# A graph network's edge counts: the first two source one-hots of seven groups made by ScalarE instead of VectorE

## The reference

```
adj  = zeros(N, N).at[src, dst].set(1)              # attention mask
cnt  = number of edges src->dst, plus the self loops # aggregation
h  = relu(layernorm(x))
x  = x + softmax(mask((h Wq + bq)(h Wk + bk)^T / sqrt(512), adj)) (h Wv + bv)
h  = relu(layernorm(x))
h  = agg(h W1 + b1);  h = relu(batchnorm(h));  h = agg(h W2 + b2)
x  = x + h            # agg(y)[s] = sum over edges s->d of dinv[s] dinv[d] y[d]
```

## Time and profile before

| what | value |
|---|---|
| three timed runs | 309.1, 309.43, 310.83 us (median 309.43) |
| profiled execution, its own time | 309.07 us |
| its span (first to last instruction) | 307.2 us |
| busy in the span | PE 295.4 us (96%), DVE 210.1 (68%), ACT 143.6 (47%), POOL 56.5 (18%) |
| source one-hots L674 | 149, 349 ns each, 44.3 us of DVE |
| chunk matmuls L1021 | 36.5 us of PE |
| granted clock of PE | 9 in all 40 slices, mean 1.000 |

### The profile page before, as it was taken

The page is one execution under the profiler, slowest core; times in us unless marked ns, Lnnn a source line. Parts: engine busy times, 40 slices in busy tenths (PEclk is TensorE's granted clock), DMA queues, the critical chain, the costliest instruction groups (busy, mean ns, idle before and its releaser), DMA issues.

```text
span 307.2 us, 4787 instructions
## 1 busy us (share of the span) xinstructions
PE 295.4 (96%) x1339; PEld 227.5 (74%) x1345; DVE 210.1 (68%) x472; ACT 143.6 (47%) x245; POOL 56.5 (18%) x94
## 2 busy tenths in 40 slices
PE   8999879899999999999999999999999999999995
PEld 6778346466565788888888888887888888878884
DVE  3798999999998648766757484667344388276311
ACT  3999924444346726635454445537623035343000
POOL 5352450000000340032121411203010044100000
PEclk9999999999999999999999999999999999999999
DMA  7815040000600308544452825223102000000221
GB/s 265 298 45 164 7 133 0 1 0 3 200 5 3 69 2 210 98 102 75 100 120 53 154 51 104 51 54 68 34 19 51 1 2 0 0 2 0 109 99 68
DMA packets 42312, 21.66 MB, mean 71 GB/s; under 512 B 35761, under 2 KB 36017, under 8 KB 42289
## 3 DMA queue, kind: packets, MB, share of 16 engines
q1 hardware_dynamic: 41744, 20.33, 26.5%
q10 hardware_dynamic: 544, 1.05, 0.9%
HBM read 10.88 MB, written 2.10 MB: 42 GB/s over the span
## 4 chain that ended last, share of the span: by engine, by line
PE 81%; DVE 7%; issue 4%; DVEq 3%; DMA 2%; ACT 1%; SPq 0%; ACTq 0%
PE ps L955 19%; PE ps L957 18%; PE ps L956 18%; PE ps L1205 10%; PE ps L1128 8%; PE ps L1021 7%; DVE src_oh L674 3%; DMA qk_raw<-L_gnn_Wq_in 2%; DVE dst_oh L676 1%; DVEq L674 1%; PE ps L989 1%; DVE T L775 0%; DVEq L666 0%; DVE smx L779 0%; DVE p L787 0%
## 5 line engine op out<-in xcount | busy, mean ns | idle before, releaser
L674 DVE TENSOR_SCALAR src_oh<-iota,ecol 128x512 f16 x149 | 44.3, 349 | 4.5 <-issue 3.4
L1021 PE MATMUL ps<-src_oh,dst_oh 128*128 x143 | 36.5, 382 | 6.2 <-DVE dst_oh L676 5.0
L1021 PEld LDWEIGHTS ps<-src_oh,dst_oh 128*128 x149 | 14.4, 104 | 25.7 <-issue 16.6
L1128 PE MATMUL ps<-cnt,qh 128*128 128x512 f32 x128 | 30.1, 391 | 0.3 <-ACT cnt L544 0.3
L1205 PE MATMUL ps<-qh,cnt 128*128 128x512 f32 x128 | 29.3, 390 | 0.0
L446 ACT ACTIVATE cnt<-ps 64x512 int16<-64x512 f32 x32 | 18.9, 591 | 20.7 <-PE ps L1035 20.3
L1128 PEld LDWEIGHTS ps<-cnt,qh 128*128 128x128 f32 x128 | 23.9, 188 | 5.6 <-DVE qh L834 0.7
L1205 PEld LDWEIGHTS ps<-qh,cnt 128*128 128x128 f32 x128 | 24.0, 188 | 5.2 <-DVE vb L936 0.3
L957 PE MATMUL ps<-v,pT 128*128 128x512 f32 x64 | 25.0, 390 | 0.0
L955 PE MATMUL ps<-hT,qh 128*128 128x512 f32 x64 | 24.9, 390 | 0.0
L955 PE MATMUL ps<-v,pT 128*128 128x512 f32 x64 | 24.9, 389 | 0.0
(11 more groups left out here) (179 smaller groups left out, 660.4 us busy)
## 6 DMA issues: line engine op xcount, KB each, us to landing
xt<-x_in SPq DMA_DIRECT2D x16, 256.0 KB, 3.3
out<-xt SPq DMA_DIRECT2D x8, 256.0 KB, 2.1
qk_raw<-L_gnn_Wk_in ACTq DMA_DIRECT2D x2, 512.0 KB, 4.7
qk_raw<-L_gnn_Wq_in SPq DMA_DIRECT2D x2, 512.0 KB, 6.5
wB_raw<-L_gnn_Wv_in SPq DMA_DIRECT2D x2, 512.0 KB, 8.5
wB_raw<-L_gnn_W_in SPq DMA_DIRECT2D x2, 512.0 KB, 3.8
w_raw<-L_gnn_W_in SPq DMA_DIRECT2D x2, 512.0 KB, 4.3
bias_row<-L_gnn_b_in SPq DMA_DIRECT2D x2, 256.0 KB, 3.7
```

The costliest lines, as they stand in the source:

```text
L674: dve.tensor_scalar(src_oh[:, bass.ds(slot, 1), j, :].rearrange("p a n -> p (a n)"), iota[:, :], ecol[:, bass.ds(c + j, 1)], None, ALU.is_ ...
L1021: m = pe.matmul(ps[:, i % 2, :], dst_oh[:, bass.ds(slot, 1), :, j].rearrange("p a n -> p (a n)"), src_oh[:, bass.ds(slot, 1), j, :].rearra ...
L1128: m = pe.matmul(bank(g), qh[:, d, a, c * P:(c + 1) * P], cnt[:, d, n * HALF:(n + 1) * HALF], start=(d == 0 and a == 1), stop=last)
```

## The change

For groups 3 to 9 the two source one-hots of the straight round are no longer made by DVE. POOL negates the source column once (`ncol`) and copies the two columns that the group needs to a fixed place (`lead_col`, after reading the group's first chunk from `lohi`). ACT makes |iota - source| for each of the two chunks, and then relu(1 - that) over both, which is 1 where they are equal and 0 elsewhere, into `lead_oh` (two buffers, in the place that `adj` takes later). It does so for group i+1 between `hi_of` of group i's items and `counts(i)`. PE waits for it (`lead_made`) before group i+1's first round. DVE still makes that round's target one-hot.

```
+ACT_LEADS = 3
+ACT_LAST = 10
...
-    adj = sb("adj", [P, ADJ, N], I16)
+    adj, lead_oh = shared([("adj", [P, ADJ, N], I16)], [("lead_oh", [P, 2, LEAD, HALF], BF16)])
+    hold("region_adj", 4)
...
+    ncol = sb("ncol", [P, NCH + PAD], F32)
+    lead_col = sb("lead_col", [P, NW, LEAD], F32)
+    ones = sb("ones", [P, 1], F32)
...
 # POOL
+        pool.memset(ones[:, :], 1.0)
...
+        def lead_columns(i):
+            bounds = pool.value_load(lohi[0:1, ORDER[i]:ORDER[i] + 1], min_val=256, max_val=257 * NCH)
+            pool.tensor_copy(lead_col[:, i, :], ncol[:, bass.ds(bounds & (NCH - 1), LEAD)]).then_inc(S["lead_cols"], 1)
...
-        pool.wait_ge(S["ecol_ready"], 1)
+        pool.wait_ge(S["ecol_ready"], 2)
...
         ln1(6)
+        pool.tensor_scalar(ncol[:, :], ecol[:, :], -1.0, 0.0, ALU.mult,
+                           ALU.add).then_inc(S["ncol_ready"], 1)
+        pool.wait_ge(S["ncol_ready"], 1)
+        pool.wait_ge(S["bounds_ready"], 1)
+        for i in range(ACT_LEADS, ACT_LAST):
+            lead_columns(i)
         for i in range(8, NW):
             targets_of(i)
...
 # ACT
+        def lead_onehots(i):
+            n = i - ACT_LEADS + 1
+            act.wait_ge(S["lead_cols"], n)
+            for j in range(LEAD):
+                act.activation(lead_oh[:, i % 2, j, :], iota[:, :], ACT.Abs,
+                               bias=lead_col[:, i, j:j + 1]).then_inc(S["lead_dist"], 1)
+            act.wait_ge(S["lead_dist"], LEAD * n)
+            act.activation(lead_oh[:, i % 2, :, :], lead_oh[:, i % 2, :, :], ACT.Relu, bias=ones[:, 0:1],
+                           scale=-1.0).then_inc(S["lead_made"], LEAD)
...
+            if ACT_LEADS <= i + 1 < ACT_LAST:
+                lead_onehots(i + 1)
             counts(i)
...
 # DVE
-            for j in range(count):
+            for j in range(count if src else 0):
...
-            chunks_of(i, first, LEAD)
+            chunks_of(i, first, LEAD, not ACT_LEADS <= i < ACT_LAST)
...
 # PE
+                              lead_oh[:, i % 2, j, :] if first and ACT_LEADS <= i < ACT_LAST else
                               src_oh[:, bass.ds(slot, 1), j, :].rearrange("p a n -> p (a n)"), start=first and j == 0,
...
+            if ACT_LEADS <= i < ACT_LAST:
+                pe.wait_ge(S["lead_made"], LEAD * (i - ACT_LEADS + 1))
```

More of the change, by code:

```diff
@@ L159, in gnn_kernel @@
     x_sums x_means x_squares ln_scale ln_coef h_ready item_ps item_hi item_lo uw_ready hw_second fill_ready
-    onehots onehots_used c_done c16 loops_added adj_in0 adj_in1 adj_in2 adj_in3
+    ncol_ready lead_cols lead_dist lead_made onehots onehots_used c_done c16 loops_added adj_in0 adj_in1 adj_in2 adj_in3
     deg_ready degm_ready degm_ps flag_ready dinv_ready
@@ L666, in bounds_of, with chunks_of @@
             return dve.value_load(lohi[0:1, ORDER[i]:ORDER[i] + 1], min_val=256, max_val=257 * NCH)
-        def chunks_of(i, c, count):
+        def chunks_of(i, c, count, src=True):
             k = dve.snap(made, min_val=0, max_val=ROUNDS)
```

## The result

The changed kernel takes 307.77 us, the kernel before 310.48 beside it (medians of 12 runs each): ratio 0.9926, 95% interval 0.9912 to 0.9940, so 2.3 us faster by the ratio (1.9 to 2.7 by its interval); 2.4 was forecast. A later comparison on another occasion gave 0.9935 (0.9914 to 0.9956), 2.0 us. Times of one kernel scatter by 1.4 to 1.9 us from run to run here, so the medians lie 2.7 us apart and the fastest runs (309.10 and 307.43) only 1.7. The profiled execution took 307.52 us, its span is 305.7.

The account below looks back on a forecast made before the run. PE was taken to bound the kernel (81% of the span), with DVE setting the pace in the windows examined. Terms 2.5 + 0.2 - 0.1 - 0.2 = 2.4 us took 309.07 to 306.7; range 305.4 to 309.6.

Parts of the forecast that it names:

- DVE's time, groups 7 to 10: DVE freed of source one-hots: PE's losses of 0.55, 0.22, 0.25 and 0.46 us in these groups go.
- the rival that DVE's sequencer sets the pace: Groups 4 to 9: DVE's sequencer is the limit, so six pairs give back only 1.2 to 1.9 us; chance 0.18.
- Group 5: Two pairs off DVE give 1.04 us of lead against PE's loss of 1.8, so the group gains 1.04.
- loss of 1.8: Group 5 before the change: its 11 chunks could close at 58.6 us but close at 60.41, PE waiting for DVE.
- The net of 0.2: POOL's preparations slide out of group 2, saving up to 0.5 us, partly taken back in groups 3 or 4; 0.2 taken.
- the ring: Group 3: DVE stands 0.72 us for PE because the ring is full, so time saved or lost before it is hidden.
- its lead in groups 6 to 9: ACT has the one-hots ready 0.7 to 0.9 us before PE reaches these groups.
- The price: ACT's three added activations per group take 0.71 + 0.71 + 1.15 = 2.57 us.
- The slope of half a microsecond for 0.1: Groups 5 to 9: each 0.1 us of ACT work per group above about 2.6 costs half a microsecond in all.
- PE's extra wait, 0.2: One more wait per group on PE's sequencer costs 0.02 to 0.05 us each, 0.2 in all.
- Behind the stage: After group 15 PE runs on nearly without a gap, so an earlier end of group 15 is an earlier end.

Follow-up runs that it names:

- two ahead: Changed kernel with a third buffer and ACT making one-hots two groups ahead; 306.41 us against 309.36 for the kernel before, ratio 0.9897.
- preparations first: Changed kernel with POOL's eight target preparations ahead of its new work and ACT's one-hots from group 4 on; 308.62 us against 309.36 before, ratio 0.9975.
- preparations early: Changed kernel with POOL's eight target preparations moved into its idle time before group 2; 307.57 us against 309.36 for the kernel before, ratio 0.9930.
- dearer ACT: Changed kernel with one more 128x1024 activation on ACT in each of the seven groups; 313.52 us against 309.42 for the kernel before, ratio 1.0122.

## Why the prediction came out

**DVE's time, groups 7 to 10: right.** Forecast were 0.55, 0.22, 0.25 and 0.46; the distances shrank by 0.47, 0.16, 0.26 and 0.42, 1.3 of 1.5. DVE's pair was worth the 0.52 that the rows gave: target one-hots follow each other without it.

```profile
49.58 0.41 DVE L707 TENSOR_TENSOR dst_oh<-iota_w,drel_first 128x256 f16 x1
49.91 0.87 DVE L705 TENSOR_SCALAR src_oh<-iota,ecol 128x512 f16 x3
```

From the target one-hot to the next source one-hot is 0.33, and where it was 49.75 for the pair and 50.27 for the target, only the latter is left. So the rival that DVE's sequencer sets the pace falls: the pairs gave back nearly what DVE's time said, and no read of the bounds shows in front of this target one-hot.

**Group 5: wrong.** The step that failed is "group 5 has 1.04 (two pairs) against a loss of 1.8, so it gains 1.04", and behind it the sentence that ACT has the one-hots "0.3 after PE reaches group 5, where DVE is later still". ACT's lateness was there, and small:

```profile
53.63 1.33 ACT L473 ACTIVATE lead_oh<-iota,lead_col 128x512 bf16<-128x512 f16 x2
55.05 1.15 ACT L476 ACTIVATE lead_oh<-lead_oh,ones 128x1024 bf16<-128x1024 bf16 x1
```

It ends at 56.20, some 0.15 after PE's transposes. But DVE was not later still: its target one-hots for the straight round and the first loop round were done at 54.89 and 56.01.

```profile
54.48 0.41 DVE L707 TENSOR_TENSOR dst_oh<-iota_w,drel_first 128x256 f16 x1
54.81 0.87 DVE L705 TENSOR_SCALAR src_oh<-iota,ecol 128x512 f16 x3
55.60 0.41 DVE L707 TENSOR_TENSOR dst_oh<-iota_w,drel_first 128x384 f16 x1
```

And a wait at the head of the group costs more than its length. PE's sequencer stands at it and prepares nothing behind it (its address work starts at 56.5); afterwards its loop rounds come 1.07 us apart, against 0.65 for the three matmuls. Ahead of groups 3, 4 and 6 to 9 an item of 12 matmuls lets the sequencer get ahead again; ahead of group 5 there are only eight transposes, 0.9 us. Two groups ahead shows it from the other side: without ACT's wait group 5 is 0.79 shorter, three quarters of the 1.04 that was forecast for this term, and the stage 1.1. The prediction's loss of 1.8 was also too large a goal: it counts group 5's chunks at 0.215 each, while in no kernel here are two of its loop rounds less than 1.07 apart. That PE's sequencer needs the 1.07 was read from rows of three kernels, not tested by changing its loop.

**POOL: mis-sized, in the kernel's favour.** The net of 0.2 was 0.32 in this trace (0.55 gained in group 2, 0.17 and 0.06 lost in groups 3 and 4). POOL's reads and copies took 0.71 to 0.73 each (one 1.11), not 1.5, so the preparations began in group 3:

```profile
38.77 0.28 POOL L370 COPY lead_col<-ncol 128x2 f32 x1 [1.03 <-issue]
39.50 0.18 POOL L370 COPY lead_col<-ncol 128x2 f32 x1 [0.45 <-issue]
...
43.65 5.51 POOL L365 TENSOR_SCALAR drel_second<-dcol 128x132 f16<-128x132 f16 x8
```

Beside them a round was up to 1.40 instead of the forecast 1.30 (1.15 and 0.15): the ring hid most of it, not all. The Trainium skill's lock (SBUF — State Buffer, "SBUF: two separate sides") would have a DVE instruction with two SBUF inputs, as the target one-hot is, stand until a POOL instruction that reads SBUF ends. These rows show less: beside POOL instructions of 0.65 to 0.78 the target one-hots lasted 0.50 to 0.52 instead of 0.41, the source one-hots up to 0.44 instead of 0.35, and DVE went on, at 0.2 to 0.25 a round. The step of 0.19 that lasted 1.22 beside DVE's `zT`, in preparations first, does look like the lock.

**ACT: right in size; its lead in groups 6 to 9 larger than forecast, and yet not free.** The price was 2.57; from the first activation's start to the last one's end it is 2.57 (53.63 to 56.20). In group 5 it was 0.15 late instead of 0.3; in groups 6 to 9 its one-hots were ready 2.1, 1.2, 1.4 and 1.3 us before PE's straight round instead of 0.7 to 0.9. Group 7:

```profile
65.44 1.15 ACT L476 ACTIVATE lead_oh<-lead_oh,ones 128x1024 bf16<-128x1024 bf16 x1
...
67.81 0.61 PE L1052 MATMUL ps<-lead_oh,dst_oh 128*128 128x512 bf16 x2
```

Against two ahead PE still lost some 0.03 to 0.08 a group. The slope of half a microsecond for 0.1 was too steep: at 3.67 a group it gives 5.4, and the stage grew by 4.25, since group 6 was mostly spared.

**PE's extra wait, 0.2: not seen** as a term of its own; groups 3 and 4 are no longer with it (6.40 and 5.70 with preparations early) than without it (6.39 and 5.68 before). **Behind the stage: right**, 205.7 us in both.

By terms the sum would read 1.3 (groups 7 to 10) + 0 (group 5) + 0.3 (POOL) + 0 (groups 11 to 15) = 1.6 instead of 2.4. That the measured gain is as forecast is partly luck: the traces show 1.6 to 1.7, and nothing on record shows a cause for the rest of the 2.3 but the scatter of the times.

## What to carry to other kernels

Work that is moved to an idle engine has to be judged by that engine's cycle in the loop and by when the result is due, and the place to look is the shortest gap, where the consumer has least to do before it asks. A wait put at the head of a short loop also costs the loop's own start: the sequencer that stands there can't prepare the rounds behind it, so making the result one step earlier may be worth as much as the move itself (two ahead gave 0.8 us more in group 5 and 1.1 in the stage). Where one engine's side work slows another on a shared path, look first for a hole in time: moving POOL's preparations to its idle time took one edit and gave 0.56 us of the stage by itself in the kernel before, 0.17 on top of the change and nothing on top of two ahead.

## What the runs showed of the hardware

- A loop round on PE with three matmuls whose addresses come from registers took 1.07 us where the sequencer had no lead, though the matmuls take 0.65; the same distance stood in the changed kernel (57.50, 58.57, 59.64), with two ahead (56.40, 57.47) and with the dearer ACT (70.02, 71.09).
- Reading one number of SBUF into a POOL register and copying two columns from the place it names took 0.71 to 0.73 us from one copy to the next, once 1.11.
- Eight POOL instructions of 128x132 lengthened DVE's round from 1.15 to 1.28 in group 2 of the kernel before and to 1.35 to 1.40 in group 3 of the changed kernel, where also the target one-hot went from 0.42 to 0.50.
- A POOL instruction of 0.19 us that started 0.05 behind a DVE tensor_tensor of 1.22 with both inputs in SBUF lasted 1.22 itself; in the three kernels where this fell on the last batch-norm coefficients, PE waited 0.6 us instead of 0.2 for what hangs on them.
